# Value products of two rounds in one burst, and three query/key slots in place of four

## What is computed

```python
# layer 0: 32 query heads of 16, one key/value head, no mask
Q = (xn @ Wq + bq).reshape(B, N, H, d_h); K = xn @ Wk + bk; V = xn @ Wv + bv
attn = softmax(einsum('bnhd,bkd->bhnk', Q, K) * scale)
out = einsum('bhnk,bkd->bnhd', attn, V).reshape(B, N, D) @ Wo + bo
# layer 1: 32 query heads, 8 key/value heads, rotary embedding, causal mask
scores = einsum('bqhd,bkhd->bhqk', rope(xq), rope(xk)) / sqrt(16), masked with the lower triangle
out = einsum('bhqk,bkhd->bqhd', softmax(scores), xv).reshape(b, s, 512) @ Wo
```

## Time and profile before

| | us |
|---|---|
| median of three runs | 2205.15 (2200.69 to 2208.09) |
| the profiled execution, its own time | 2202.45 |
| its span, first to last instruction | 2200.7 |
| attention of layer 0, first score to last value product | 536.9 to 1292.8 |
| attention of layer 1 | 1604.3 to 2134.2 |
| PE, DVE, ACT busy in the whole span | 2020.8, 1459.4, 1102.1 |

### The profile page before, as it was taken

How to read it: one execution, slowest core, us unless ns; L and a number is a source line. 1 busy time by engine, 2 the same in 40 slices (tenths; PEclk the granted TensorE clock), 3 DMA queues, 4 the chain that set the end, 5 groups by cost and what they waited for, 6 DMA issues and landing times.

```text
span 2200.7 us, 29316 instructions
## 1 busy us (share of the span) xinstructions
PE 2020.8 (92%) x11120; PEld 949.3 (43%) x11120; DVE 1459.4 (66%) x1896; ACT 1102.1 (50%) x2130; POOL 144.8 (7%) x135
## 2 busy tenths in 40 slices
PE   3999999998999999999999986898899999999987
PEld 2878787732222222222222245543433443443436
DVE  7444444437888888888888718339777777777733
ACT  2221211132777777777777742112156666666660
POOL 4000000041000000000000103004200000000010
PEclk7999999997999999999999998999789999999999
DMA  5010100034111112111120121103311211213123
GB/s 172 21 32 12 39 1 0 0 85 106 24 24 27 24 25 43 24 26 25 24 67 19 34 81 52 37 19 98 99 38 32 48 37 35 48 32 80 33 69 118
DMA packets 91747, 99.66 MB, mean 45 GB/s; under 512 B 20033, under 2 KB 71425, under 8 KB 91617
## 3 DMA queue, kind: packets, MB, share of 16 engines
q1 hardware_dynamic: 91616, 97.92, 17.3%
HBM read 69.36 MB, written 27.98 MB: 44 GB/s over the span
## 4 chain that ended last, share of the span: by engine, by line
PE 78%; DVE 14%; DMA 4%; ACT 2%; issue 2%; SPq 1%; POOL 0%; ACTq 0%; DVEq 0%
PE ps L1069 17%; PE ps L1087 16%; PE ps L1051 15%; DVE arena L808 6%; PE ps L869 6%; PE ps L870 6%; PE ps L871 6%; PE ps L987 3%; PE ps L943 3%; DMA arena<-inverse 2%; PE ps L1054 1%; DVE arena L788 1%; ACT arena L607 1%; PE ps L1090 1%; PE ps L934 1%
## 5 line engine op out<-in xcount | busy, mean ns | idle before, releaser
L808 DVE TENSOR_REDUCE arena<-ps 128x1 f32<-128x1024 f32 (+7 forms) x1024 | 976.1, 988 | 261.7 <-PE ps L1054 131.6
L607 ACT ACTIVATE arena<-ps 128x512 f32<-128x512 f32 (+3 forms) x1792 | 892.2, 554 | 389.3 <-PE ps L1087 225.3
L1087 PE MATMUL ps<-arena 98*128 98x512 bf16 (+3 forms) x1792 | 570.0, 361 | 11.0 <-ACT arena L607 6.1
L1051 PE MATMUL ps<-arena 96*128 96x512 bf16 (+3 forms) x1792 | 532.3, 369 | 30.7 <-DVE arena L808 25.1
L1069 PE MATMUL ps<-arena 128*17 128x512 f32 (+3 forms) x3584 | 431.6, 553 | 1.1 <-ACT arena L607 1.1
L1087 PEld LDWEIGHTS ps<-arena 98*128 98x128 bf16 x1792 | 162.5, 97 | 486.3 <-ACT arena L607 372.6
L1051 PEld LDWEIGHTS ps<-arena 96*128 96x128 bf16 x1792 | 163.5, 99 | 214.9 <-DVE arena L808 91.9
L869 PE MATMUL ps<-x_hi,w_hi 128*128 128x512 f32 (+1 forms) x480 | 195.5, 407 | 52.6 <-DVE x_lo L835 31.3
L538 ACT ACTIVATE xn<-ps 128x512 f32<-128x512 f32 (+1 forms) x44 | 26.3, 598 | 275.3 <-PE ps L871 275.3
L870 PE MATMUL ps<-x_lo,w_hi 128*128 128x512 f32 (+1 forms) x352 | 140.5, 399 | 0.0
L871 PE MATMUL ps<-x_hi,w_lo 128*128 128x512 f32 (+1 forms) x352 | 140.2, 398 | 0.0
(11 more groups left out here) (114 smaller groups left out, 1594.6 us busy)
## 6 DMA issues: line engine op xcount, KB each, us to landing
qparts<-arena SPq DMA_DIRECT2D x96, 128.0 KB
arena<-qparts SPq DMA_DIRECT2D x64, 192.0 KB, 3.7
arena<-qparts SPq DMA_DIRECT2D x64, 128.0 KB, 4.0
numer<-arena SPq DMA_DIRECT2D x256, 32.0 KB
xnT<-numer SPq DMA_DIRECT2D x16, 512.0 KB
arena<-inverse SPq DMA_DIRECT2D x16, 512.0 KB
arena<-kparts SPq DMA_DIRECT2D x192, 32.0 KB, 2.9
w_raw<-in_wgu SPq DMA_DIRECT2D x20, 256.0 KB, 3.6
```

What stands on the lines that cost most here:

```text
L607: act.activation(prob[local % P_RING][:, q0:CH], bank(local % SP_RING)[:, q0:CH], ACT.Exp, scale=SCALE).then_inc(S["p_ready"], 1)
L808: dve.tensor_reduce(maxes[c][:, h * TPC + qt:h * TPC + qt + 1], src[:, 0:max_width(l == 1, c, qt)], AX_X, ALU.max).then_inc(S["x_done"], 1)
L1051: last = pe.matmul(dst[:, k0:k1], q_slot[u][0:ROWS, c, h, qt * P:(qt + 1) * P], k_slot[u][0:ROWS, k0:k1], start=True, stop=not diag)
L1087: mm = pe.matmul(bank(slot)[:, q0:CH], k_slot[u][0:ROWS + MROWS, kt * P:(kt + 1) * P], q_slot[u][0:ROWS + MROWS, c, h, q0:CH], start=True, ...
```

## The change

`PQ` goes from 2 to 4, so the ring holds 16 probability tiles, and a new constant `BURST = 2` makes PE take two quads one behind the other, in every second round. To make room for eight more tiles of 512 columns there are three query/key/value slots in place of four, loaded two groups ahead. The output-weight split by ACT moves from the first half of the last group to the second, since its place was tied to the length of the ring. The loops over `it` and `u` become one loop over groups `n`. The arena is laid out anew.

```diff
-SLOTS = 4
-ITERS = B * NG // SLOTS
-SP_RING, PQ = 3, 2
+SLOTS = 3
+GROUPS = B * NG
+SP_RING, PQ = 3, 4
 P_RING = PQ * HG
 BURST_AT = 2
+BURST = 2
...
@@ SP
-                def step(it, u, last):
-                    n = it * SLOTS + u
-                    final = last and u == SLOTS - 1
-                    if not (last and u > 0):
-                        v = (u + SLOTS - 1) % SLOTS
+                for n in range(GROUPS):
+                    u, v = n % SLOTS, (n + 1) % SLOTS
+                    if n == GROUPS - 4:
+                        load_output(l, 0)
+                    if n == GROUPS - 2:
+                        load_inverses(l, 0)
+                    final = n == GROUPS - 1
+                    if n + SLOTS - 1 < GROUPS:
                         sp.wait_ge(S["pv_done"], n * group_quads[l] + PQ)
-                        load_slot(l, it if u == 0 else it + 1, v)
+                        load_slot(l, n + SLOTS - 1)
...
@@ ACT
-                                if n == B * NG - 1 and c == 0 and i >= P_RING and i % 2 == 0 and (i - P_RING) // 2 < KC:
-                                    k = (i - P_RING) // 2
+                                if n == GROUPS - 1 and c == QC - 1 and i % 2 == 0 and i // 2 < KC:
+                                    k = i // 2
                                     act.activation(wo_hi[:, k, :], w_o[:, k, :], ACT.Copy).then_inc(S["wo_hi_done"], 1)
...
@@ PE
-                                if h == BURST_AT and len(pending) > HG:
-                                    pv_quad()
+                                if h == BURST_AT and len(pending) > BURST * HG:
+                                    for _ in range(BURST):
+                                        pv_quad()
```

More of the change, by code:

```diff
@@ L106, in build @@
         bias_o = sb("bias_o", [P, D])
-        v_all = sb("v_all", [P, B * NG, KT, DH + 1])
+        v_all = sb("v_all", [P, GROUPS, KT, DH + 1])
         ident = sb("ident", [P, P])
@@ L189, in build @@
         inv = [region(H * N // P) for _ in range(B)]
-        den = [[], [region(N) for _ in range(KC)]]
-        den[0].append(region(N))
-        assert used[0] <= projection_end
+        den = [[region(N)], [arena[:, (KC + i) * N:(KC + i + 1) * N] for i in range(KC)]]
+        assert 2 * KC * N <= P_RING * CH and used[0] <= projection_end
         used[0] = projection_end
@@ L195, in build @@
         res = [den[0][i][:, 0:D] for i in range(4)]
-        q_slot = [region(HG * N // 2, BF16).rearrange("p (c h q) -> p c h q", c=QC, h=HG) for _ in range(SLOTS)]
-        k_slot = [region(N // 2, BF16) for _ in range(SLOTS)]
+        LAST = (GROUPS - 1) % SLOTS
+        q_slot, k_slot = [None] * SLOTS, [None] * SLOTS
+        slot_order = [u for u in range(SLOTS) if u != LAST]
+        for u in slot_order:
+            q_slot[u] = region(HG * N // 2, BF16).rearrange("p (c h q) -> p c h q", c=QC, h=HG)
+        for u in slot_order + [LAST]:
+            k_slot[u] = region(N // 2, BF16)
+        q_slot[LAST] = region(HG * N // 2, BF16).rearrange("p (c h q) -> p c h q", c=QC, h=HG)
         v_slot = [region(KT * (DH + 1)).rearrange("p (k d) -> p k d", k=KT) for _ in range(SLOTS)]
@@ L306, in store_parts, with load_slot @@
                             sp.dma_start(dst, src).then_inc(S["q_out"][m], 16)
-            def load_slot(l, it, u):
+            def load_slot(l, n):
                 S = L[l]
-                n = it * SLOTS + u
+                u = n % SLOTS
                 q = qparts[l][n * HG:(n + 1) * HG, :, :]
-                kn = n if l else it // (ITERS // B)
+                kn = n if l else n // NG
                 k = kparts[l][kn:kn + 1, :, :]
@@ L329, in max_rows, with store_o @@
                                  negm[c][0:NX, s, :]).then_inc(S["m_in"][c], 16)
-            def store_o(l, it, u, c):
+            def store_o(l, n, c):
                 S = L[l]
-                n = it * SLOTS + u
                 sp.wait_ge(S["o_copied"], n * QC + c + 2)
@@ L345, in attention @@
                     sp.wait_ge(S["q_out"][m], 16 * PARTS * QC)
-                load_slot(l, 0, 0)
+                load_slot(l, 0)
                 store_parts(l, 1)
-                for u in range(1, SLOTS - 1):
-                    load_slot(l, 0, u)
+                for n in range(1, SLOTS - 1):
+                    load_slot(l, n)
                 for m in range(NQ):
@@ L353, in attention @@
                     max_rows(l, 0, c, c)
-                def step(it, u, last):
-                    n = it * SLOTS + u
-                    final = last and u == SLOTS - 1
-                    if not (last and u > 0):
-                        v = (u + SLOTS - 1) % SLOTS
+                for n in range(GROUPS):
[6 more added lines that the diff above has]
+                    if n + SLOTS - 1 < GROUPS:
                         sp.wait_ge(S["pv_done"], n * group_quads[l] + PQ)
-                        load_slot(l, it if u == 0 else it + 1, v)
+                        load_slot(l, n + SLOTS - 1)
                     if TAIL[l]:
                         max_rows(l, u, 1, n * QC + 1)
-                        store_o(l, it, u, 0)
+                        store_o(l, n, 0)
                     if not final:
-                        max_rows(l, (u + 1) % SLOTS, 0, (n + 1) * QC)
+                        max_rows(l, v, 0, (n + 1) * QC)
                     if not TAIL[l]:
-                        store_o(l, it, u, 0)
+                        store_o(l, n, 0)
                         if not final:
[L370 to L381, removed]
+                            max_rows(l, v, 1, (n + 1) * QC + 1)
+                    store_o(l, n, 1)
                 load_output(l, 1)
@@ L473, in _ @@
                 pool.wait_ge(S["v_done"], V_STEPS[l])
[L475 to L478, removed]
                 pool.wait_ge(S["lo_done"], NCH * NQ)
[L481 to L486, removed]
+                for n in range(GROUPS):
+                    if n >= SLOTS:
+                        pool.wait_ge(S["pv_done"], (n - SLOTS + 1) * group_quads[l] + PQ)
+                    pool.tensor_copy(v_slot[n % SLOTS], v_all[:, n if l else n // NG, :, :]).then_inc(S["v_slot_ready"], 1)
                 for t in range(KC):
@@ L600, in attend @@
                     before = None
-                    for n in range(B * NG):
+                    for n in range(GROUPS):
                         for c in range(QC):
@@ L824, in invert @@
                     dve.reciprocal(inv[b], inv[b]).then_inc(S["inv_ready"], 1)
-                for n in range(1, B * NG - 2):
+                for n in range(1, GROUPS - 2):
                     maxima(n)
                 invert(0)
-                maxima(B * NG - 2)
-                maxima(B * NG - 1)
+                maxima(GROUPS - 2)
+                maxima(GROUPS - 1)
                 def low(c):
@@ L1071, in pv_quad @@
                         mm.then_inc(S["pv_done"], 1)
-                    for n in range(B * NG):
+                    for n in range(GROUPS):
                         u = n % SLOTS
-                        has_next = n < B * NG - 1
+                        has_next = n < GROUPS - 1
                         pe.wait_ge(S["v_slot_ready"], n + 1 + SLOTS)
@@ L1113, in _ @@
                 attend()
-                pe.wait_ge(S["o_copied"], B * NG * QC + 1)
+                pe.wait_ge(S["o_copied"], GROUPS * QC + 1)
                 pe.wait_ge(S["wo_ready"], 1)
```

## The result

The changed kernel takes 2242.74 us (median of 4, 2239.56 to 2244.45), the kernel before 2202.92 in the same comparison: a ratio of 1.0176, interval 1.0152 to 1.0199. It is 40 us slower. The profiled execution has a span of 2237.8 us against 2200.7.

What follows compares the result with a forecast made beforehand. PE's order was taken to set the time, with DVE close behind in layer 0. Layer 0 +41, layer 1 -11.5 and the split +3 gave +32.5 on 2202.45, so 2235, predicted as 2238 us; range 2212 to 2266.

Steps and rivals of the forecast that it cites:

- The sign and its cause: Whole kernel: slower, since four maxima tiles between merged bursts wait for DVE's two buffers in layer 0; over 0.3% slower at 0.86.
- The transitions into and out of a burst: PE in both attentions: merging two bursts saves 0.20 us per pair of rounds, 45 us in all, with passes 0.44 apart.
- The stepped pair of 5.90 us: Layer 0, plain pair of rounds stepped: 5.90 us against 5.65, with waits of 0.17 and 0.27 for DVE's buffers.
- The group of layer 0: Layer 0 attention: a group takes 49.6 us against 47.0, with 5.7 of waiting; sixteen groups cost +41 us.
- the split: ACT's output-weight split, moved to a half without maxima pieces: +1 and +2 us in the two layers, ends 0 and 4.
- Layer 1: Layer 1 attention: a group becomes 0.7 us shorter, sixteen 11.5, with bounds of -19 and +7.
- Three slots, the ring, the layout: Slot loads by SP: costed at nothing, with a cover of 11 us; rival of late slots, with the clock, at 0.02.
- The sum: Whole kernel: 41 - 11.5 + 3 = +32.5 us on the profiled execution's 2202.45, so 2235.
- Maxima stay hidden: Rival: PE's pieces wait for DVE no more than before, giving 2173 us; decided at a reduction pitch of 1.06; chance 0.08.
- The second quad at full price: Rival: a merged burst's second quad costs like its own burst, nothing saved, +44 on the forecast, 2282 us; chance 0.07.
- the clock as I priced it: Rival: PE's waits drop both attentions' granted clock to 0.89, costing 120 us; chance 0.02 together with late slots.

## Why the prediction was right

*The sign and its cause.* Both held. The transitions into and out of a burst are saved as worked out: passes 0.433 apart where I took 0.44. The stepped pair of 5.90 us came out at 5.88, with waits of 0.18 and 0.25 where I had 0.17 and 0.27. Over a group PE waits 6.0 us where the stepping had 5.7. The rule on draining that the Trainium skill states (TensorEngine Tiling (Array Packing), Key Properties) holds here in its direction, 0.31 into a burst and 0.55 out of it, but says nothing of what the longer burst does to DVE.

*The group of layer 0.* Predicted 49.6, seen 49.7. The whole attention grew by 44.4 us from first to last score (753.7 to 798.1) where I had 42 with the split. Groups 14 and 15 together grew by 5.3, what two groups at 2.7 give, but unevenly, by 0.2 and 5.1. The rest is in one group that I had not stepped through: DVE takes the reciprocals of the first batch in group 13 (L815), right behind a transposition. The timelines of DVE and of PE there:

```profile
1201.58 1.75 DVE L815 RECIPROCAL arena<-arena 128x256 f32<-128x256 f32 x1 [0.15 <-DVE arena L807]
1203.25 3.52 DVE L799 TENSOR_REDUCE arena<-ps 128x1 f32<-128x1024 f32 x3
```

```profile
1201.54 0.61 PE L1042 MATMUL ps<-arena 96*128 96x512 bf16 x2
...
1204.47 1.04 PE L1042 MATMUL ps<-arena 96*128 96x512 bf16 x2 [1.89 <-DVE arena L799]
...
1208.65 0.39 PE L1078 MATMUL ps<-arena 98*128 98x512 bf16 x1
```

Between the pieces' starts at 1201.54 and 1204.47 PE does one tile's two pieces and two scores, and waits 1.89 us. Before, a group with the reciprocals was 48.0 us against 47.0, with a wait of 0.84 at the pieces; now it is 52.9 against 49.7. Half of these 3.2 us is the clock. It falls to half at 1204.47, where PE starts again. From there two pieces, a score, a burst and the step to the next score take 4.18 us, to 1208.65; the same run at full clock takes 2.60 (742.74 to 745.34). The term was missing, 2.2 us: 1.6 of clock, and 0.6 of waiting for DVE, which has no slack now.

*Layer 1.* Predicted 32.6 a group, seen 32.5. From first to last score it fell by 7.7 us (528.8 to 521.1) where the sum had 9.5 with the split: again the reciprocals (group 13 went from 34.3 to 35.0), and a last group 3.7 us longer, where I allowed 2 for the split. Both hold a stretch at half clock, 2074.90 and 2153.30 above; with single bursts the last group is 1.8 us longer. I had the waits of a group for DVE fall by 0.2; those of the weight loads rose by 0.5, which does not decide it, since they partly overlap PE's work.

*Three slots, the ring, the layout.* Costed at nothing. The kernel with single bursts shows it: both groups as before, and 0.14% in all, of which about 2 us are the split in layer 1.

*The sum.* +32.5 on the profiled execution; the spans differ by 37.1. Of the missing 4.6, 2.4 are in layer 0 and 1.8 in layer 1. The clock can account for most of them: 17 us of the attentions ran at half clock against 3.4 before, and half of the difference, 7 us, is the most that this can have cost. That is an estimate from these rows; I had put the term at nothing. Between the medians the kernel lost 39.8. My median of 2238 is nearer to 2242.74 than 39.8 is to 32.5, and that is luck: it started from 2205, and the kernel before then measured 2203.

*The rivals.* "Maxima stay hidden" was decided by the pitch of a reduction, and the halved reductions show that the order of merged and single does turn in an undisturbed group, if not in layer 0 as a whole. The point itself, 1.06 us, was not tried. But the fast case was priced too high: PE's work fell by 45 us, and against the single bursts with the same reductions only 6 us remained (2177.97 against 2183.8), all of them in layer 1. In layer 0 ACT and the last group take the gain back. The second quad at full price is ruled out by the rows above. So is the clock as I priced it, at 120 us; but the mechanism is there, in the short stretches of this kernel and in the fall to 0.92 of layer 1 with the tail. I had also read the slices too well: the one that holds layer 1's first 47 us reads 8.

## What to carry to other kernels

A long uninterrupted run on the engine that sets the time saves its own transitions, and can starve the engines that it feeds: before merging two runs, compare the work that a consumer has left at the run's start with the time until it gets more. Here DVE had 1.46 us left when the burst began at 743.49, and its next reduction started only at 746.20, 2.71 us later; the difference is its 1.25 us of idle time, and PE waits for it afterwards. Then step through one period with the steps of the trace; where that reproduces the old period it can be believed for the new one, but only for the waits whose rules it holds (it had no DMA queue, and was 91 us out when one mattered). Look also at what a wait does to the clock behind it. And try the order of the fill-in work before its grouping: here places alone gave 23 us in layer 0, where the merge had cost 44.

## What the runs showed of the hardware

Fp32 products that are 17 columns wide, four side by side, ran in passes 0.433 us apart for as long as only such passes followed, also from one quad to the next with other weights and with a wait on a semaphore between them in the code; the change from and to full-width bf16 products cost about 0.2 us for both ways together.

The granted clock fell to half behind single waits of PE that were short: behind one of 1.89 us for DVE (1204.47 in the changed kernel) and behind one of 2.25 us for a DMA (1776.70 in the run with a tail in layer 1). The steady waits of layer 0, 6.0 us in each group of 49.7 and 0.2 to 0.9 us at a time, left it at 0.99.
